# Attention worked by query tiles, or by key tiles with a row of minus the maximum and a column of ones

## The reference

```python
q = (x @ Wq.T + bq).reshape(B, T, H, HD);  k = ...;  v = ...
logits = einsum('bthd,bshd->bhts', q, k) * HD ** (-0.5)
logits = where(tril(ones((T, T))), logits, -inf)
att = softmax(logits, axis=-1)
o = einsum('bhts,bshd->bthd', att, v).reshape(B, T, D)
```

## Time and profile before

| | us |
|---|---|
| median of three runs | 3831.18 |
| the profiled execution | 3832.34 |
| its span, first to last instruction | 3830.6 |
| main loops of the four attentions, first score to last value sum | 321.4, 251.1, 320.3, 318.4 |
| granted TensorE clock, whole span, share of full speed | 0.907 |

### The profile page before, as it was taken

One profiled execution on the slowest core, in us unless ns is written; L12 is line 12 of the kernel. 1 busy time (PEld: TensorE's weight loads), 2 busy tenths in 40 slices (PEclk: granted clock), 3 DMA queues, 4 the chain that ended last, 5 costly groups with the idle time before them and its releaser, 6 DMA issues. The chain is left out here.

```text
span 3830.6 us, 46962 instructions
## 1 busy us (share of the span) xinstructions
PE 2985.5 (78%) x16238; PEld 2308.6 (60%) x16238; DVE 2146.5 (56%) x3614; ACT 1609.9 (42%) x3492; POOL 996.3 (26%) x967
## 2 busy tenths in 40 slices
PE   0035767999748991879999568887999889998797
PEld 0011217788545761457777457676888778887686
DVE  6114673688532112567777625773588746886443
ACT  0000004677413541534444324662477636775322
POOL 4776650366413432043333000000000000001220
PEclk9767988999868995989999769998999999999899
DMA  1125654433146982254443144413522034221222
GB/s 58 43 62 141 191 171 149 120 60 57 35 136 211 345 285 84 122 179 124 128 121 89 55 166 126 86 29 117 146 48 51 20 114 122 51 60 37 81 72 81
DMA packets 234092, 418.76 MB, mean 109 GB/s; under 512 B 48902, under 2 KB 146356, under 8 KB 229890
## 3 DMA queue, kind: packets, MB, share of 16 engines
q1 hardware_dynamic: 177490, 278.85, 24.4%
q0 software_dynamic: 56368, 136.93, 13.2%
HBM read 323.98 MB, written 95.49 MB: 110 GB/s over the span
## 5 line engine op out<-in xcount | busy, mean ns | idle before, releaser
L927 DVE TENSOR_TENSOR at_s<-at_pb,at_s 125x500 fp32r<-125x500 f32 (+1 forms) x864 | 482.3, 584 | 190.7 <-ACT at_s L840 190.2
L840 ACT ACTIVATE at_s<-at_pb 125x500 fp32r<-125x500 f32 (+1 forms) x864 | 447.8, 519 | 272.1 <-PE at_pb L757 269.4
L757 PE MATMUL at_pb<-ident,at_p 125*125 125x125 f32 x2880 | 478.0, 281 | 32.6 <-ACT at_p L855 14.8
L757 PEld LDWEIGHTS at_pb<-ident,at_p 125*125 125x125 f32 x2880 | 418.2, 190 | 128.4 <-DVE at_s L927 70.9
L774 PE MATMUL at_pb<-at_s,at_v 125*128 125x250 f32 x2880 | 483.4, 296 | 7.6 <-DVE t_t L939 3.9
L917 DVE TENSOR_REDUCE at_max<-at_pb 125x1 f32<-125x1250 f32 (+4 forms) x320 | 423.1, 1322 | 12.4 <-PE at_pb L742 7.7
L855 ACT ACTIVATE at_p<-at_pb,at_max 125x1250 f32<-125x1250 f32 (+4 forms) x320 | 382.7, 1196 | 30.0 <-DVE at_max L917 28.7
L774 PEld LDWEIGHTS at_pb<-at_s,at_v 125*128 125x128 f32 x2880 | 382.9, 191 | 14.3 <-DVE at_s L927 7.2
L1974 ACT ACTIVATE g_hot<-g_plain,g_edges 128x125 f32<-128x125 f32 x704 | 223.1, 388 | 253.3 <-PE g_pm L1958 241.9
L1346 PE MATMUL g_ps<-g_got,g_hot 128*125 128x512 f32 x336 | 181.1, 637 | 142.0 <-DMA g_got<-support,g_edges 108.9
L1921 POOL DMA_INDIRECT g_got<-nodes,g_edges x176 | 166.4, 945 | 442.6 <-DVE g_msg L2004 269.6
(11 more groups left out here) (276 smaller groups left out, 5376.2 us busy)
## 6 DMA issues: line engine op xcount, KB each, us to landing
w_ring<-in_L_ffn_w SPq DMA_DIRECT2D x128, 512.0 KB, 11.0
at_shared<-k_parts SPq DMA_DIRECT2D x64, 312.5 KB
ml_w<-in_mlp_w SPq DMA_DIRECT2D x64, 256.0 KB
k_parts<-at_shared SPq DMA_DIRECT2D x64, 250.0 KB, 3.3
q_parts<-at_shared SPq DMA_DIRECT2D x64, 250.0 KB, 3.1
h_edges<-em_both SPq DMA_DIRECT2D x11, 1024.0 KB, 3.8
g_h<-h_edges SPq DMA_DIRECT2D x11, 1024.0 KB, 6.6
at_shared<-q_parts SPq DMA_DIRECT2D x32, 312.5 KB
```

What stands on the lines that cost most here:

```text
L757: ins = pe.transpose(pturn[0:TN, g % 2, TN * (t % 4):TN * (t % 4) + TN], p[:, u % 2, TN * t:TN * t + TN], c.ident[0:TN, 0:TN])
L840: act.activation(p_hi[:, u // 2 % 2, 4 * n:4 * n + m, TN * (u % 2):TN * (u % 2) + TN], pturn[0:TN, g % 2, 0:TN * m].rearrange("p (a b) -> ...
L927: dve.tensor_tensor(p_lo[at], pturn[0:TN, g % 2, 0:TN * m].rearrange("p (a b) -> p a b", b=TN), p_hi[at].bitcast(F32), ALU.subtract).then_ ...
```

## The change

The attention's main loop is written anew; the same edit reaches all four. Blocks take the place of units: a block is one head and one of three chunks of queries (500, 500, 250: four, four and two tiles), 24 per attention.

- For each query tile one score pass against the keys' high part alone, in the old arrangement (queries on the partitions), of which only minus the maximum is kept (`rough_scores`, `largest`). There is one buffer for it, three banks wide.
- The maxima of a block are turned into one row by transposes of a 125x1 column (`turn_max`), and ScalarE copies that row into partition 64 of a second moving operand (`keep_max`).
- The scores are computed by key tiles (`scores`): the stationary tile is 125 keys, the queries of the block move, in two fp32r matmuls. The second of them has the keys' low part in 64 rows, and a row of ones that meets the row of minus the maximum.
- ScalarE takes the exponential from PSUM into `p` in float32, already with keys on the partitions. There are no turns of the probabilities and no high and low part of them.
- The value sums (`values`) are full-width float32 matmuls: 125 keys by 125 queries of `p` are stationary, and 65 columns move: 64 of v and one of ones, which gives the sum. Each block's sums are begun by a bfloat16 matmul of zeros.
- VectorE inverts the sums and scales (`scale`); the output is turned by transposes (`turn_out`) and copied into `out_t` by ScalarE (`keep_out`). The inverse no longer goes through DRAM, and GpSimd multiplies nothing.
- Heads are loaded one at a time (six transfers each) instead of in pairs (twelve).
- In the causal attention keys are cut to the exact tile, and the diagonal tile is masked twice: in the rough pass and in the key tile.
- The first attention's 160 indirect transfers: 20 ahead of the loads of k, 20 ahead of those of q, 120 behind them with nothing in between.
- The output weights are read into place when the last key tile's scores are done.
- v is kept in float32 and copied by VectorE alone; three fills of 2500 columns are added on VectorE ahead of the first projection item.

```diff
+                def rough_scores(b, k):
+                    ...
+                    if maxed_by(b) + k >= 1:
+                        pe.wait_ge(max_ready, maxed_by(b) + k)
+                    for a in range(0, TN * seen(i), 512):
+                        e = min(a + 512, even(TN * seen(i)))
+                        ins = pe.matmul(score[:, a:e], q_first[:, m, TN * i:TN * i + TN], k_first[:, m, a:e], start=True, stop=True)
+                    ins.then_inc(scored, 1)
+                def turn_max(b):
+                    pe.wait_ge(max_ready, maxed_by(b + 1))
+                    if b >= 2:
+                        pe.wait_ge(kept, b - 1)
+                    for k in range(len(tiles[b])):
+                        ins = pe.transpose(pmisc[0:1, TN * k:TN * k + TN], neg_max[:, b % 2, k:k + 1], c.ident[0:TN, 0:TN])
+                    ins.then_inc(max_turned, 1)
+                def scores(b, t):
+                    h, lo, hi = blocks[b]
+                    m, g, a = h % 2, turns_by(b) + t, since(b, t) // 2 * 2
+                    if t == 0:
+                        pe.wait_ge(max_in, b + 1)
+                    if g >= ST:
+                        pe.wait_ge(exp_done, g - ST + 1)
+                    pe.matmul(pst[g % ST][:, a - lo:hi - lo], k_first[:, m, TN * t:TN * t + TN], q_first[:, m, a:hi],
                               start=True, stop=False)
+                    pe.matmul(pst[g % ST][:, a - lo:hi - lo], k_second[:, m, TN * t:TN * t + TN], q_second[:, m, a:hi],
+                              start=False, stop=True).then_inc(turned, 1)
+                def values(b, t):
+                    ...
+                        pe.matmul(pout[b % 2][:, 0:m * (HD + 1)], nil[:, 0:TN], nil[:, 0:m * (HD + 1)], start=True, stop=False)
+                    pe.wait_ge(exp_done, g + 1)
+                    for k, i in enumerate(tiles[b]):
+                        if t < seen(i):
+                            ins = pe.matmul(each(b)[:, k, :], p[:, g % PR, TN * k:TN * k + TN], v[:, t, h, :], start=False, ...)
+                    ins.then_inc(valued, 1)
+                for g, (b, t) in enumerate(order):
+                    scores(b, t)
+                    for k in rough_at(b, t):
+                        rough_scores(b + 1, k)
                     if g >= 2:
+                        values(*order[g - 2])
+                    if b >= 1 and t == min(5, keys[b] - 1):
+                        turn_out(b - 1)
+                    if t == keys[b] - 1 and b + 1 < NB:
+                        turn_max(b + 1)
+                    # ScalarE, for the same (b, t)
+                    act.activation(p[:, g % PR, a - lo:hi - lo], pst[g % ST][:, a - lo:hi - lo], ACT.Exp).then_inc(exp_done, 1)
+                    ...
+                    if t == keys[b] - 1 and b + 1 < NB:
+                        keep_max(b + 1)
+                # SyncE, behind the loads of the heads
+                sp.wait_ge(turned, turns_by(NB))
+                sp.wait_ge(early_in, 16)
+                sp.dma_start(w_out.bitcast(F32), wo_d).then_inc(early_in, 16)
```

More of the change, by code:

```diff
@@ L538, in attention @@
[L538 to L554, removed]
-            top, low = slice(0, 64), slice(64, 128)
[L556 to L564, removed]
+        RINGS, ST, PR = 4, 2, 4
@@ new lines, in attention @@
+        neg_max = sb("at_max", [TN, 2, 4])
+        inverse = sb("at_inv", [TN, 2, 4])
+        flat = sb("at_flat", [128, 2])
+        nil = sb("at_nil", [TN, 4 * (HD + 1)], BF16)
+        bank = main.enter_context(nc.psum_tensor(f"at_pb_{nc.next_id()}", [128, 8, 512], F32))
+        p = w_raw[0:TN, :, :, :].rearrange("p a k n -> p (a k n)").rearrange("p (r q) -> p r q", r=PR)
+        score = bank[0:TN, 0:3, :].rearrange("p a b -> p (a b)")
+        pst = [bank[0:TN, 3 + n, :] for n in range(ST)]
@@ L589, in attention @@
[L589 to L594, removed]
+        blocks = [(h, *CHUNKS[n]) for h in range(HEADS) for n in range(3)]
+        NB = len(blocks)
+        tiles = [range(lo // TN, hi // TN) for _, lo, hi in blocks]
+        keys = [(hi // TN if causal else NT) for _, lo, hi in blocks]
@@ new lines, in attention @@
+        since = lambda b, t: max(blocks[b][1], TN * t) if causal else blocks[b][1]
+        even = lambda n: (n + 1) // 2 * 2
+        seen = lambda i: i + 1 if causal else NT
+        maxed_by = lambda b: sum(len(tiles[x]) for x in range(b))
+        turns_by = lambda b: sum(keys[:b])
+        diagonal = lambda b, t: causal and t in tiles[b]
+        order = [(b, t) for b in range(NB) for t in range(keys[b])]
+        masks_by = lambda g: sum(1 for x in order[:g] if diagonal(*x))
+        rough_at = lambda b, t: [k for k in range(len(tiles[b + 1]) if b + 1 < NB else 0)
+                                 if k * max(keys[b] - 2, 1) // len(tiles[b + 1]) == t]
@@ new lines, in turn_out @@
+                def turn_out(b):
+                    pe.wait_ge(scaled, b + 1)
+                    pe.wait_ge(max_in, min(b + 2, NB))
+                    for k in range(len(tiles[b])):
+                        ins = pe.transpose(pmisc[0:HD, TN * k:TN * k + TN], o_row[:, b % 2, k, :], c.ident[0:TN, 0:TN])
+                    ins.then_inc(out_turned, 1)
+                pe.wait_ge(set_up, 7)
+                pe.wait_ge(first_in, 64 * LOADS)
+                pe.wait_ge(low, len(items) - 3)
+                for k in range(len(tiles[0])):
+                    rough_scores(0, k)
@@ L795, in _ @@
+                for x in order[-2:]:
+                    values(*x)
+                turn_out(NB - 1)
             @block.scalar
@@ L866, in _ @@
+                keep_out(NB - 1)
             @block.vector
@@ L941, in _, with largest @@
-                dve.wait_ge(added, NU // 2)
+                def largest(b, k):
+                    n, w = maxed_by(b) + k + 1, TN * seen(tiles[b][k])
+                    dve.wait_ge(scored, n)
+                    if k == 0 and b >= 2:
+                        dve.wait_ge(max_turned, b - 1)
+                    if causal:
+                        late = score[:, w - TN:w]
+                        dve.tensor_tensor(late, late, c.causal[:, 0:TN], ALU.add).then_inc(masked, 1)
+                        dve.wait_ge(masked, n)
+                    dve.tensor_reduce(neg_max[:, b % 2, k:k + 1], score[:, 0:w], AX, ALU.max, negate=True).then_inc(max_ready, 1)
@@ L943, in attention @@
+                for k in range(len(tiles[0])):
+                    largest(0, k)
+                for b, t in order:
+                    if diagonal(b, t):
+                        cut_future(b, t)
+                    for k in rough_at(b, t):
+                        largest(b + 1, k)
+                    if b >= 1 and t == min(3, keys[b] - 1):
+                        scale(b - 1)
+                scale(NB - 1)
         main.close()
```

327 lines of the change are left out of this document (118 added, 209 removed).

## The result

The changed kernel takes 4011.86 us (median of four runs, 4007.32 to 4015.43) where the kernel before, on the same chip, takes 3829.47: ratio 1.047, interval 1.046 to 1.049. It is slower, as forecast, and 4015 was within 0.1%. By stage it was not that close: the plain loops were forecast 46 us too long and the causal one 49 us too short, and that these two cancelled is luck.

A forecast was written before the change was run, and what follows sets the result against it. TensorE was taken to bound the loops, by its work and the waits in its order. Profiled 3832.3 + 186 (plain loops) + 7 (causal) - 16 (ends) + 6 (beginning) = 4015 us; range 3860 to 4130.

The forecast's parts named there:

- The plain loops: Main loops of three of the four attentions: 382 us against 320, +62 a loop, +186 for three.
- The causal loop: Main loop of the causal attention: 258 us against 251.1, +7, with bounds from -25 to +40.
- Value records: Full-width float32 value products: the stationary load sets the cost, 200 records a head at 0.1125 us, 22.5 us.
- The row of maxima: At each block's start TensorE waits for ScalarE's copy: 0.9 us, 0.7 in a two-tile block, 2.5 us a head.
- The rough chain: Rough passes share one buffer, 2.35 us from pass to pass; uncovered in the two-tile block, 1.2 us a head.
- Start and drain: Each plain loop's beginning and end: 9.5 us of start, 3 for a fallen clock, 1 of draining.
- the rival of the clock: TensorE's granted clock falls: at half clock for a tenth of the work +34 us a loop, 4140 us; chance 0.12.
- The ends: After each loop's last product: the first falls from 22.2 to 6 us, -16; the other three stay.
- The rest: Beginning of each attention: six transfers of q by head pair instead of four, 1.5 us each time, +6.
- cheap products: Rival: the stationary load does not set the value products' cost; a record is 0.060 us, -298, 3717 us; chance 0.05.
- 0.081 us a record: Rival, the skill's figure for a matmul with its load: value records cheaper by 179 us, 3836, no change; chance 0.03.
- Covered waits: Rival: the new waits are covered, -36 us a plain loop, -40 in the causal: 3867, still slower; chance 0.12.

The follow-up runs named there:

- early: Changed kernel with the next block's maxima turned and copied one key tile earlier, in blocks of 8 and 10 key tiles; 3955.0 us (1.032).
- max500: Changed kernel with the rough pass and its maximum covering only the first 500 keys, and the exponential scaled by 0.1; 3879.2 us (1.012).
- ahead: Changed kernel, causal attention only: rough passes spread further apart, output's scaling, turn and copy earlier in the short block, no matmul added or removed; 3951.4 us (1.030).
- both: Changed kernel with the schedules of early and ahead together; 3892.2 us (1.015).

## Why the prediction was right, and where it was not

**What bounds.** Right: TensorE's work and the waits in its own order. VectorE and ScalarE fell to 129 and 148 of 367 us and gave nothing back.

**The plain loops, +62 forecast, +46 to +49 measured.** A head takes 44.2 us (749.59 to 793.80, from one block's start to the same block of the next head) instead of 46.0.
- Value records: cause (the stationary load) and size were right: 200 x 0.109 = 21.8 us by head, 22.5 forecast. The experts' record of 0.1125 had 128 stationary columns, three more. The Trainium skill ("TensorE: Matmul & The Clock Gate", "LDWEIGHTS (loading the stationary operand)") gives a load as its columns over 1.2 in ns, 104 ns for 125 columns and 53 for 63. The traces agree at full clock, some 5 ns above both: 0.109 and 0.057 us. At the lower clock a record takes 0.213 us, which that figure doesn't cover.
- Scores: taken as pure stream, 11.5 us, and so measured: a key tile is 8 x 0.109 and 0.46 (above).
- The row of maxima: 1.25 less 0.35, what four turns take where nothing waits (775.18 to 775.53), is 0.9 us, 2.5 a head with the two-tile block, as forecast; `early` took 2.2 to 2.3 of them.
- The rough chain: 1.2 us a head forecast, 0.3 measured by `max500`, and 0.5 by what TensorE's loads waited for maxima in the first loop (3.5 us between 730 and 1030 us).
- Start and drain: 367.1 less eight heads of 44.2 is 13.4 us, 13.5 forecast; the clock was low in it, 0.56 over the 14.0 us to the first key-tile scores.

The forecast was 1.8 us a head too high, 15 a loop, 46 in three. The mis-sized terms are the rough chain (0.7 to 0.9 us of it) and the value record (0.7); the rest is spread over smaller ones.

**The causal loop, +7 forecast, +56 measured.** This is the step that failed. Its waits were forecast well (6.9 us a head, 38.0 in seven heads or 5.4 measured). The clock was not: the rival of the clock said of the causal loop that it "kept 0.96, so I expect it held". It had been kept by other work, though with as much waiting. In the new loop, with waits of 1.2 and 1.5 us in each head's first block, it didn't hold: `ahead` shows 37 us for it. With the maxima's waits gone and the clock at 0.94 the loop takes 240, within the bounds of the forecast (226 to 291). The rival of the clock had the mechanism and the price (34 us a loop), but I gave it to all loops alike; it struck the one with the short blocks. The Trainium skill ("TensorE: Matmul & The Clock Gate", "A second HAM failure mode: psum-queue depth-cycling"), cited there, tells of a clock that swings where TensorE idles briefly between groups of products. The trace of the new causal loop agrees, at 0.76; that of the old one, with as much waiting at 0.96, does not.

**The ends, -16 forecast, -28 measured.** The first gave 18.7. The other three gave 3 each, which I had put at nothing ("lay beside the loop"): behind the last value sum there had stood the inverse's round trip by DRAM and GpSimd's multiplication, and these were on the path. In the fourth loop before, from the copy at 3507.88 to the next stage at 3514.22:

```profile
3511.40 0.72 POOL L679 TENSOR_TENSOR s_t<-s_t,at_all 128x250 f32<-128x250 f32 x1 [11.45 <-DMA at_all<-inverse]
```

That was 6.3 us; from the output's copy to the next stage it is 3.3 now.

**The rest**, +6 forecast and measured, was not taken apart by a run. The forecast was 1.5 us ahead of each loop; the traces have +0.7, +1.5, +0.4 and +3.5 ahead of the four and +0.2 behind the last. So the sum came out and its parts didn't.

Of the rivals, cheap products were wrong, and 0.081 us a record as well. Covered waits is what `both` came to by another order: 58 us over the kernel before, where 35 were worked out.

## What to carry to other kernels

Where a matmul holds a large stationary tile and moves few columns, price it by the stationary columns, from the distance between loads inside a run; a run's length over its number of records misprices it, since both ends overlap with what stands beside them. Don't count a smaller stationary tile as a gain before a trace shows it among its neighbours: here four fifths of it went in loads that no longer ran beside the products. Look for waits of a microsecond on TensorE where blocks are short: in the causal loop here they cost 28 us by their length and 37 more in clock, and spreading the passes that wait (65 us) was worth more than taking work away (30 us in max500). When a rewrite has gains that don't depend on each other, test each alone in the old kernel: here one index expression and one of four loops were worth having.

## What the hardware showed that was not expected

Less work made the kernel slower: with 33 instead of 65 moving columns in the value products the causal loop went from 305.7 to 399.1 us, at a granted clock of 0.54 instead of 0.76. And more work made it faster: 160 products on zeros, placed in two of its waits, took it to 270.5 us, at 0.94. And a stationary tile of half the columns halved the load, from 0.109 to 0.057 us, but cut a key tile only from 1.33 to 1.25 us.
